# Two of the four block sums of a square layer's activations moved from VectorE to GpSimd, with turned signs, and the weights' check spread over one more tile

## The reference

```python
h = jax.nn.silu(_tlin(x, w1_w, w1_s)) * _tlin(x, w2_w, w2_s)
h = jax.nn.gelu(_tlin(h, h1_w, h1_s), approximate=False)
h = jax.nn.gelu(_tlin(h, h2_w, h2_s), approximate=False)
return _tlin(h, w3_w, w3_s)
```

## Time and profile before

| | us |
|---|---|
| median of 3 runs (1295.19 to 1295.3) | 1295.23 |
| the profiled execution, timed | 1296.77 |
| its span in the profile | 1295.0 |
| PE busy | 1284.7 (99%) |
| DVE busy | 974.9 (75%) |
| POOL busy | 800.2 (62%) |
| ACT busy | 762.0 (59%) |

### The profile page before, as it was taken

One profiled execution on the slowest core, in us unless ns is written; L12 is line 12 of the kernel. 1 busy time (PEld: TensorE's weight loads), 2 busy tenths in 40 slices (PEclk: granted clock), 3 DMA queues, 4 the chain that ended last, 5 costly groups with the idle time before them and its releaser, 6 DMA issues.

```text
span 1295.0 us, 16588 instructions
## 1 busy us (share of the span) xinstructions
PE 1284.7 (99%) x6066; PEld 1065.8 (82%) x6066; DVE 974.9 (75%) x1239; ACT 762.0 (59%) x1012; POOL 800.2 (62%) x804
## 2 busy tenths in 40 slices
PE   8999999999999999999999999999999999999997
PEld 7788888888888888888888888888888888888887
DVE  7888778778787777868777787777878777556675
ACT  4566655666556665565655656557565566555664
POOL 7964015999669995699947999388984890040000
PEclk9999999999999999999999999999999999999999
DMA  9698935455254541654416454265432644213441
GB/s 336 260 370 243 295 116 169 162 165 176 78 171 161 169 163 70 182 172 152 163 73 196 152 177 135 82 191 173 157 130 86 210 156 146 99 66 130 139 159 47
DMA packets 98199, 209.62 MB, mean 162 GB/s; under 512 B 14144, under 2 KB 17472, under 8 KB 97088
## 3 DMA queue, kind: packets, MB, share of 16 engines
q1 hardware_dynamic: 80176, 157.11, 36.2%
q0 software_dynamic: 17936, 51.39, 12.7%
HBM read 175.92 MB, written 38.83 MB: 166 GB/s over the span
## 4 chain that ended last, share of the span: by engine, by line
PE 98%; DVE 1%; ACT 0%; issue 0%; POOL 0%; POOLq 0%
PE ps L791 63%; PE ps L691 18%; PE ps L846 9%; PE ps L756 4%; PE ps L742 1%; PE ps L826 0%; PE ps L815 0%; PE ps L804 0%; PE ps L819 0%; PE ps L807 0%; PE ps L823 0%; PE ps L812 0%; PE ps L862 0%; DVE split L1330 0%; PE ps L680 0%; PE ps L880 0%
## 5 line engine op out<-in xcount | busy, mean ns | idle before, releaser
L791 PE MATMUL ps<-split,ring 128*128 128x512 f32 x3584 | 815.4, 389 | 0.0
L791 PEld LDWEIGHTS ps<-split,ring 128*128 128x128 f32 x3584 | 672.7, 188 | 139.7 <-DVE split L1324 0.4
L1324 DVE TENSOR_TENSOR split<-quad,split 128x1024 fp32r<-128x1024 f32 x224 | 290.4, 1305 | 143.3 <-ACT split L955 142.3
L955 ACT ACTIVATE split<-quad 128x1024 fp32r<-128x1024 f32 x224 | 231.5, 1052 | 42.1 <-PE ps L791 42.1
L691 PE MATMUL ps<-xT,w 128*128 128x512 f32 x1024 | 236.3, 391 | 1.0 <-ACT xT L1041 0.8
L691 PEld LDWEIGHTS ps<-xT,w 128*128 128x128 f32 x1024 | 190.9, 188 | 42.8 <-DVE quad L1318 2.0
L1000 ACT ACTIVATE quad<-quad,cols 128x512 f32<-128x512 f32 x192 | 136.5, 719 | 65.6 <-DVE quad L1355 38.0
L1347 DVE TENSOR_TENSOR quad<-quad 128x1024 f32<-128x1024 f32 x128 | 173.2, 1394 | 0.0
L537 POOL TENSOR_TENSOR ry<-ry,s 128x256 f32<-128x256 f32 x56 | 40.7, 759 | 200.7 <-issue 115.3
L938 ACT ACTIVATE rows<-ps,cols 128x512 f32<-128x512 f32 x128 | 87.2, 687 | 92.9 <-PE ps L691 47.2
L1318 DVE SCALAR_TENSOR_TENSOR quad<-ps,cols,rows 128x512 f32<-128x512 f32 x128 | 94.4, 745 | 47.4 <-ACT rows L938 30.7
(11 more groups left out here) (162 smaller groups left out, 1245.0 us busy)
## 6 DMA issues: line engine op xcount, KB each, us to landing
ring<-hs SPq DMA_DIRECT2D x428, 256.0 KB, 3.6
xin<-in_x SPq DMA_DIRECT2D x16, 512.0 KB, 4.2
s_h<-s SPq DMA_DIRECT2D x16, 512.0 KB, 4.5
seen<-in_h POOLq DMA_DIRECT2D x64, 128.0 KB, 2.9
ry<-in_x SPq DMA_DIRECT2D x15, 512.0 KB, 5.0
out<-ry SPq DMA_DIRECT2D x15, 512.0 KB, 2.6
z_h<-xin POOLq DMA_DIRECT2D x56, 128.0 KB, 3.8
xT<-z_h POOLq DMA_DIRECT2D x14, 512.0 KB, 6.5
```

Of the source, the lines that this page charges most:

```text
L791: mm = e.matmul(ps[:, 4 * (w % 2) + m, :], ring[n % RING][:, m * P:(m + 1) * P], slot[:, k, g, :], start=first and k == 0 and g == 0, stop ...
L955: e.activation(both(slots[i][:, :, 0, :], g), both(quad[at[t][L][name]], g), ACT.Identity).then_inc(hi, 1)
L1324: e.tensor_tensor(both(slots[i][:, :, 1, :], g), both(quad[at[t][L][FAST[w][1]]], g), both(slots[i][:, :, 0, :], g).bitcast(F32), ALU.subt ...
```

## The change

- The sums `t3` and `t4` leave DVE's program. POOL adds them in a new function, `add_late`, two instructions of 128x1024 each, and tells ACT by four new semaphores `late_sum`. It waits for the first sum of the layer (for `t3`) or the low halves of `t2` (for `t4`), since it writes over a piece that was read there, and for the blocks that it adds.
- All four sums are additions now. The signs that this turns are taken up in the weights' pieces (two operations of `fold_round`) and in two of DVE's steps after a product (`product_out`).
- `subtract` becomes `add_up` and is called for `t1` and `t2` alone; `n_sum` counts four instead of eight.
- `count_good` takes 14 chunks a tile instead of 16, in four parts between the additions, and four chunks are left for the last tile.

```diff
-CHUNKS_A_TILE = 16
+CHUNKS_A_TILE = 14
...
+        late_sum = {n: [sem(f"sum_{n}{g}") for g in range(2)] for n in ("t3", "t4")}
...
-                e.tensor_tensor(a22, a21, a22, ALU.add).then_inc(folded, 1)
+                e.tensor_tensor(a22, a21, a22, ALU.subtract).then_inc(folded, 1)
...
-                e.tensor_tensor(a12, a12, a11, ALU.subtract).then_inc(folded, 1)
+                e.tensor_tensor(a12, a12, a11, ALU.add).then_inc(folded, 1)
...
+            def add_late(t, L, name):
+
+                src = {"t3": "b22", "t4": "b21"}[name]
+                for g in range(2):
+                    if name == "t3":
+                        on.wait_ge(block_sum, n_sum(t, L, 0, g))
+                        if L == 0:
+                            on.wait_ge(gated, n_gate(2 * t + 1, Q + 2 * g + 1))
+                        else:
+                            on.wait_ge(gelu["b22"], n_block(t, 0, 2 * g + 1))
+                    else:
+                        on.wait_ge(lo, n_split(t, L, 2, g))
+                        if L == 0:
+                            on.wait_ge(gated, n_gate(2 * t, Q + 2 * g + 1))
+                        else:
+                            on.wait_ge(gelu["b21"], n_block(t, 0, 2 * g + 1))
+                    dst, src_ = both(quad[at[t][L][name]], g), both(quad[at[t][L][src]], g)
+                    e.tensor_tensor(dst, src_, dst, ALU.add).then_inc(late_sum[name][g], 1)
...
-                    count_good(CHUNKS_A_TILE * (t - 1), CHUNKS_A_TILE * t)
+                begin = CHUNKS_A_TILE * (t - 1)
+                if t:
+                    parts = (begin, begin + 2, begin + 6, begin + 8, begin + CHUNKS_A_TILE) if t < END else (begin, begin + 4)
+                    add_late(t, 0, "t3")
+                    count_good(parts[0], parts[1])
+                    add_late(t, 0, "t4")
+                    if t < END:
+                        count_good(parts[1], parts[2])
+                    add_late(t, 1, "t3")
+                    if t < END:
+                        count_good(parts[2], parts[3])
+                    add_late(t, 1, "t4")
+                    if t < END:
+                        count_good(parts[3], parts[4])
                 if t == 0:
-                    for n in range(RING, 2 * NW * Q):
+                    n = RING
+                    for L, w, name in ((0, 0, "t3"), (0, 2, "t4"), (1, 0, "t3"), (1, 2, "t4")):
+                        while n < min((L * NW + w) * Q + RING, 2 * NW * Q):
+                            feed_raw(n)
+                            n += 1
+                        add_late(t, L, name)
+                    while n < 2 * NW * Q:
                         feed_raw(n)
+                        n += 1
...
             def high(t, L, w, g):
...
-                if name[0] == "t":
+                if name in ("t1", "t2"):
                     on.wait_ge(block_sum, n_sum(t, L, int(name[1]) - 1, g))
+                elif name in ("t3", "t4"):
+                    on.wait_ge(late_sum[name][g], 2 * t + L + 1)
...
-                e.tensor_tensor(dst, a, b, ALU.subtract).then_inc(block_sum, 1)
+                e.tensor_tensor(dst, a, b, ALU.add).then_inc(block_sum, 1)
...
-                                elif w == 0:
-                                    subtract(t, 0, 2, m - 2)
-                                elif (w == 2 if t == 0 else w == 1) and m >= 2:
-                                    subtract(t, 0, 3, m - 2)
                                 elif w == NW - 1 and m >= 2:
-                                    subtract(t, 1, 0, m - 2)
+                                    add_up(t, 1, 0, m - 2)
```

More of the change, by code:

```diff
@@ L233, in n_sum @@
         def n_sum(t, L, i, g):
-            return (2 * t + L) * 8 + 2 * i + g + 1
+            return (2 * t + L) * 4 + 2 * i + g + 1
         def n_gate(h, m):
@@ L543, in add_y @@
                     e.tensor_tensor(res[:, b, :], res[:, b, :], yt[:, b, :], ALU.add).then_inc(pool_out, 1)
+            def add_late(t, L, name):
[15 more added lines that the diff above has]
+                    e.tensor_tensor(dst, src_, dst, ALU.add).then_inc(late_sum[name][g], 1)
             chunks = [w_kpm[n][:, k, c:c + COUNT] for n in ("h1", "h2", "w1", "w2", "w3")
                       for k in range(w_kpm[n].shape[1]) for c in range(0, w_kpm[n].shape[2], COUNT)]
-            assert len(chunks) * COUNT * P == WEIGHTS and len(chunks) <= CHUNKS_A_TILE * (NT - 2)
+            assert len(chunks) * COUNT * P == WEIGHTS and len(chunks) <= CHUNKS_A_TILE * (NT - 2) + 4
             def count_good(first, last):
@@ L1331, in low_last, with add_up @@
                                 both(slots[i][:, :, 0, :], g).bitcast(F32), ALU.subtract).then_inc(last_lo, 1)
-            def subtract(t, L, i, g):
+            def add_up(t, L, i, g):
                 for name in SUMS[i][1:]:
@@ L1357, in product_out @@
                     on.wait_ge(u3_kept, n_block(t, L, m))
-                    e.tensor_tensor(quad[t1][:, m, :], ps[:, Q + m, :], quad[t1][:, m, :], ALU.add).then_inc(c_sum["b22"], 1)
+                    e.tensor_tensor(quad[t1][:, m, :], ps[:, Q + m, :], quad[t1][:, m, :], ALU.subtract).then_inc(c_sum["b22"], 1)
                 elif w == 5:
@@ L1361, in product_out @@
                     on.wait_ge(u2_kept, n_block(t, L, m))
-                    e.tensor_tensor(quad[b11][:, m, :], here, quad[b11][:, m, :], ALU.add).then_inc(c_sum["b12"], 1)
+                    e.tensor_tensor(quad[b11][:, m, :], here, quad[b11][:, m, :], ALU.subtract).then_inc(c_sum["b12"], 1)
             def sums_of_proj():
@@ L1517, in _ @@
                     low(t, 0, 1, 1)
-                    subtract(t, 0, 0, 0)
-                    subtract(t, 0, 0, 1)
+                    add_up(t, 0, 0, 0)
+                    add_up(t, 0, 0, 1)
                 for L in range(2):
@@ L1533, in _ @@
                                     if t == 0:
-                                        subtract(t, 0, m, 0)
-                                        subtract(t, 0, m, 1)
+                                        add_up(t, 0, m, 0)
+                                        add_up(t, 0, m, 1)
                                     elif m == 0:
-                                        subtract(t, 0, 1, 0)
-                                        subtract(t, 0, 1, 1)
-                                elif w == 0:
-                                    subtract(t, 0, 2, m - 2)
-                                elif (w == 2 if t == 0 else w == 1) and m >= 2:
-                                    subtract(t, 0, 3, m - 2)
+                                        add_up(t, 0, 1, 0)
+                                        add_up(t, 0, 1, 1)
                                 elif w == NW - 1 and m >= 2:
-                                    subtract(t, 1, 0, m - 2)
+                                    add_up(t, 1, 0, m - 2)
                             elif w == 0 and m >= 2:
-                                subtract(t, 1, 1, m - 2)
-                            elif (w, m) in ((1, 2), (2, 2)):
-                                subtract(t, 1, 2, w - 1)
-                            elif (w, m) in ((2, 3), (3, 2)):
-                                subtract(t, 1, 3, w - 2)
+                                add_up(t, 1, 1, m - 2)
                             if 0 < t < END and L == 0 and w in (2, 3) and m >= 2:
```

## The result

The changed kernel takes 1317.43 us (median of four executions, 1316.21 to 1317.78), the kernel before 1295.26 us beside it (four, 1295.19 to 1295.72). The ratio is 1.0167 with a 95% interval of 1.0152 to 1.0182: slower by 22 us. I had forecast 1304.4 us, with 1298.6 to 1311.5 as the range. The direction was right, and the size was too small by more than half.

What follows compares the result with a forecast made beforehand. The prediction took PE, busy 1284.7 of 1295.0 us, as the bound; 6.2 us in tile 0 plus 3.0 in tiles 1 to 6 gave 9.2 us on the median 1295.2, so 1304.4 us, range 1298.6 to 1311.5.

Steps and rivals of the forecast that it cites:

- the 1.09 us of the rows: Tile 0 before the change: each DVE split held up 1.09 us by POOL's 512-column steps; low end for 1024 columns.
- The fold's last issue at 83.5: Tile 0: POOL's last weight-fold store is issued at 83.5 instead of 86.4, 2.9 us earlier, and the t3 additions follow.
- the first rival: No change: POOL's fold in tile 0 ends by 79.5, so t3 is in time; 1295.3 us, chance 0.07.
- the rival of that name: POOL runs over: checks don't get shorter, y's gating comes late, perhaps 2 us a tile; 1313 us, chance 0.06.
- the first low half, asked for at 87.0, is blocked until 88.3: Tile 0, layer 1, fifth product: DVE's first t3 low half waits only for POOL's second t3 addition, ending at 89.4.
- waits for nothing by then: Tile 0: POOL's first t4 addition is ready and takes the ports between DVE's two low halves, 89.4 to 91.6.
- My upper bound of 9.1 for the tile: Tile 0: PE's wait at the fifth product is 9.1 us if POOL's fold saves nothing.
- I add nothing: Tile 0: no row shows how TensorE's clock answers a pause of 6 us, so nothing is added for it.
- the rest of tile 0 is covered: Tile 0 after the fifth product: t4 ready at 95, due at 107; layer 2's additions stand behind POOL's feeds.
- 6 x 0.5 = 3.0: Tiles 1 to 6: additions blocking low halves cost 0.5 us a tile, between ends of 0 and 1.2, 3.0 us together.
- a window of 1.2 us: Steady tiles, layer 2's second product: an addition must begin within 1.2 us of 428.1 to make PE wait 1.0 us.
- Every pair collides: Additions meet low halves in the worst phase at all three places of a tile; at half, 1318 us, chance 0.14.

Runs made afterwards that it cites:

- steps of 256 columns: Changed kernel with tile 0's sums back on DVE and each later addition cut in four steps of 128x256 without waits between them: 1295.44 us, ratio 0.9996.
- one kernel above: Changed kernel with only layer 1's t3 additions of tiles 1 to 7 left on POOL, the other sums back on DVE: 1295.93 us, ratio 1.0002.
- the kernel with chained additions: Changed kernel, but in tile 0, layer 1, each t4 addition waits for POOL's own addition before it: 1314.89 us, ratio 1.0151.

## Why the prediction was wrong in size

**Right.** PE had no slack to give and DVE's relief bought nothing: the sign. The duration of an addition, 2.4 us alone (2.33 to 2.42 measured) and 3.3 beside DVE (3.20 to 3.40). The hold of 2.2 us for 1024 columns (2.19 measured). I had set the Trainium skill's rule of an exclusive lock (SBUF — State Buffer, section "SBUF: two separate sides") against the 1.09 us of the rows, and the trace agrees with the rule: a low half that meets the start of an addition waits nearly its whole length (2.19 us of 2.4). The fold's last issue at 83.5 (measured 82.97), and with it the fall of the first rival. The place of the long wait, layer 1's fifth product in tile 0. POOL's sums of the steady tiles in time, and the two checks fewer as the room for them: with 16 checks POOL does run over, at 2.3 us a stage, where the rival of that name had 2 us.

**Wrong, first step: tile 0, 6.2 us against 12.9.** The step that failed is "the first low half, asked for at 87.0, is blocked until 88.3", with which DVE takes its turn when the second addition ends. It was asked for at 86.5 and blocked until 92.3. POOL's additions had all that they needed, and the second of `t3` and both of `t4` kept it out. I had written that the first `t4` addition "waits for nothing by then", and yet gave DVE the turn before it. The rows from which I took the taking of turns (82.06 of DVE, 78.90 and 83.37 of POOL) are of fold steps that each wait for the one before; in them POOL's next step had something to wait for. The kernel in which they wait for one another has the predicted pause (5.6 us in the list of waits, 6.2 forecast) and takes 1314.89 us; in the changed kernel it is 8.5. My upper bound of 9.1 for the tile was made of POOL saving nothing, and did not have this in it. The second part is "I add nothing" for the clock: 1.7 us of matmuls at 0.50 after the pause. The Trainium skill (TensorE: Matmul & The Clock Gate, Part 1) says that TensorE's clock is halved when it has been idle and comes back under load; here the trace agrees, with 0.50 in the row that follows the pause and 1.00 in the next. The third is "the rest of tile 0 is covered". The second product of layer 2 was late by 1.4 us, by the very collision that I had priced for the steady tiles, and another 0.8 us went behind it; the kernel with only the first `t3` given back shows what is left without the pause and its clock, 3.9 us with a weight piece that lands late.

**Wrong, second step: steady tiles, 3.0 us against 9.6.** The mechanism was right, as steps of 256 columns show by taking all of it away. The term "6 x 0.5 = 3.0" was mis-sized, in two ways. First, I gave a wait to one place of a tile, layer 2's second product. There are three: layer 1's `t4` costs something in four tiles, and layer 2's `t4`, of which I had asked only whether it would be in time, falls upon the low halves of the fifth product in tiles 1, 3, 4 and 5. Second, I took one timetable of POOL for all tiles, good to 2 us, and gave a window of 1.2 us the chance of a random phase. But POOL's two checks before layer 1's `t4` took from 10.0 us (tile 6) to 14.9 us (tile 1), where I had counted 12.8 to 13.8, so that `t4` begins 16.3 to 22.2 us into the layers and not at 20.5. With that the product that is hit changes (the fourth in tiles 3 and 5; the fifth, which I had passed with 0.4 us to spare, in tiles 1 and 4; layer 2's second alone in tiles 2 and 6), and all six tiles are hit somewhere, for 0.9 to 2.6 us. Four of them lose more than the 1.2 us of my upper end. Nor is the phase random: tiles 2 and 6 lose 0.9 us each, tiles 3 and 5 1.65 each, and the four executions of the changed kernel lie within 1.6 us.

The rival "Every pair collides", at half of its worst case, had 1318 us, beside 1317.43 measured. Its reason was right as far as every steady tile is hit. That its number fits is luck: it is 6.2 for tile 0 and 17 for the others, which measured 12.9 and 9.6, and the two errors nearly cancel. I gave it 0.14 and left it out of the range.

Why DVE is kept out in tile 0 and takes turns in tile 3 is open. Whole additions and steps of 256 columns behave alike in that, so the length of an instruction is not it. A wait between POOL's instructions lets DVE in, yet in tile 3 close steps do so too. Nor is it tile 0 as such: in the changed kernel, layer 2's `t3` additions of tile 0 (from 119.53) meet two low halves that wait for one addition each.

```profile
120.39 6.75 DVE L1366 TENSOR_TENSOR split<-quad,split 128x1024 fp32r<-128x1024 f32 x2
```

Two differences stand in the traces. DVE had been idle for 8.3 us before the low half that was kept out, and for 3.9 us at most before any other that met one of the changed kernel's additions. And the DMA engines were fully busy from 82.99 to 93.40 (share 1.00), against 0.56 from 119.50 to 126.20 and 0.44 from 624.70 to 631.60. A kernel with only one of these changed was not tried.

## What to carry to other kernels

Moving 64 two-input SBUF operations from DVE to GpSimd did not relieve DVE here, since DVE had such work too (974.9 us busy before, 977.9 after). Before such a move, for each addition list which DVE operations fall beside it, and what PE is due then, at every product and not at the tightest alone. If it must be moved, put it where DVE is idle (the fourteen whole additions of one kernel above, twelve of them there, cost nothing) or cut it into steps of 256 columns (9.8 us of loss became none), and look twice at a run of such additions, with no wait between them, ahead of a DVE operation that PE awaits. In a program that repeats, a narrow window isn't a small chance times many tiles: the tiles are not independent, the window drifts from one to the next, and here it hit some product in all six. The case in which every tile is hit belongs in the range.

## What the runs showed of the hardware that I had not expected

- POOL's instructions in a row can keep a waiting DVE operation out for longer than one of them: 6.88 us over three additions of 1024 columns, 8.16 us over eleven steps of 256 (tile 0). In the steady tiles DVE took its turn after one: no low half there took more than 3.42 us in the changed kernel.
- A pause of PE costs more than its length. After pauses of 3.9 to 9.1 us, in five kernels, the granted clock was 0.50 and a matmul of 512 columns took some 0.4 us instead of 0.2275 (13 in 5.69 us behind the pause of 8.4, eight in 3.05 us behind that of 9.1); in the kernel with chained additions, whose pause was 5.6 us, this is the row behind it, six matmuls in 2.45 us. Where waits were 1.7 us at most, the mean granted clock stayed at 0.998 to 0.999.

```profile
93.15:95.60 2.45, 2.45 (x6) 1.97 (x7) 0.50 1.01 381
```

- DVE's busy share is no measure of its work: 64 sums fewer, and 3 us more busy time.
